# One run of 32 tiles for two attention layers with the feed-forward cut into its steps, in a gated cross-attention kernel

## What is computed

```python
x = x + tanh(g_xattn[0]) * L0_xattn(layernorm(x), ctx)        # 16 heads of 8, 77 keys, then norm, gelu FFN 512, norm
x = x + tanh(g_ffn[0])   * L0_ffn(layernorm(x))               # DEPTH = 2 local attention layers, below
x = x + tanh(g_xattn[1]) * L1_xattn(layernorm(x), ctx, trans) # 8 heads of 16, scores * trans, masked softmax
x = x + tanh(g_ffn[1])   * L1_ffn(layernorm(x))               # bf16 -> fp8 rounding, 128x128 product, bias

def _layer(x):                      # one of the two local layers, 8 heads of 64
    q, k, v = split(shift_token(x) @ wqkv)          # half of the features come from the token before
    q, k = rotary_xpos(l2norm(q) * qs, l2norm(k) * ks)
    x = x + local_attention(q, k, v) @ wo           # window of 64, looking one window back
    h = layernorm(shift_token(x)) * lg + lb
    a, g = split(h @ w1 + b1)                       # 2 * 341 hidden
    return x + (a * gelu(g)) @ w2 + b2
```

## Time and profile before

| | |
|---|---|
| median of 3 runs | 737.69 us (737.4, 740.5, 737.69) |
| the profiled execution | 737.42 us, its span 735.6 us |
| busy: PE, DVE, ACT, POOL | 584.8, 506.6, 346.6, 417.7 us |
| stage A ends, first `products` | 203.2 us |
| local layers end (last `finish`) | 591.6 us |
| second cross attention, to its last sum | 591.5 to 696.8 us |
| rounded feed-forward | 698.4 to 735.6 us |

### The profile page before, as it was taken

The page is one execution under the profiler, slowest core; times in us unless marked ns, Lnnn a source line. Parts: engine busy times, 40 slices in busy tenths (PEclk is TensorE's granted clock), DMA queues, the critical chain, the costliest instruction groups (busy, mean ns, idle before and its releaser), DMA issues. The chain is left out here.

```text
span 735.6 us, 13205 instructions
## 1 busy us (share of the span) xinstructions
PE 584.8 (79%) x4922; PEld 412.7 (56%) x4922; DVE 506.6 (69%) x1117; ACT 346.6 (47%) x603; POOL 417.7 (57%) x342
## 2 busy tenths in 40 slices
PE   4679999689289999998699899999968955768511
PEld 3337777557136777777465466777754623555400
DVE  1868888646777888875644778888655336676496
ACT  2235554363356666664534566566535323343221
POOL 5536674272289999990312999999513015555320
PEclk9559999979698999999999999999999966789955
DMA  7600000000011111110000111111100000000001
GB/s 254 182 1 1 1 1 1 1 1 1 0 43 29 31 31 31 40 29 2 1 1 14 30 47 30 32 30 32 24 1 1 1 0 0 0 1 1 1 0 57
DMA packets 16141, 18.15 MB, mean 25 GB/s; under 512 B 4261, under 2 KB 10831, under 8 KB 16079
## 3 DMA queue, kind: packets, MB, share of 16 engines
q1 hardware_dynamic: 14639, 14.70, 7.8%
q10 hardware_dynamic: 1440, 2.61, 1.1%
HBM read 8.01 MB, written 1.05 MB: 12 GB/s over the span
## 5 line engine op out<-in xcount | busy, mean ns | idle before, releaser
L222 POOL TENSOR_TENSOR rstd<-rstd,minus_half 128x4 f32<-128x4 f32 x32 | 34.1, 1065 | 162.6 <-DVE rstd L216 162.6
L1295 POOL TENSOR_TENSOR qk<-qk 128x512 f32<-128x512 f32 x64 | 80.2, 1274 | 33.8 <-DVE qk L1181 33.8
L1299 POOL TENSOR_TENSOR rn<-n,minus_half 128x16 f32<-128x16 f32 x32 | 93.8, 2931 | 2.7
L1178 DVE TENSOR_TENSOR qk<-ps,rt 128x512 f32<-128x512 f32 x64 | 44.0, 688 | 45.1 <-ACT sq L1099 31.2
L1137 ACT ACTIVATE ptb<-ps 128x512 f32<-128x512 f32 x64 | 34.8, 595 | 72.5 <-PE ps L902 72.5
L1304 POOL TENSOR_TENSOR qk<-qk,rn 128x512 f32<-128x512 f32 x64 | 65.4, 1044 | 2.5
L610 POOL TENSOR_TENSOR xy<-xy,rd 128x616 f32<-128x616 f32 x32 | 38.9, 1217 | 39.9 <-DVE rd L479 39.9
L1099 ACT ACTIVATE sq<-ps 128x512 f32<-128x512 f32 x64 | 37.7, 598 | 20.8 <-PE ps L865 7.6
L1423 POOL TENSOR_TENSOR vv<-vv,mx 128x616 f32<-128x616 f32 x16 | 19.9, 1243 | 44.5 <-DVE mx L1385 44.5
L563 PE MATMUL ps<-pt,vbd_a 128*128 128x128 f32 x320 | 39.5, 279 | 6.8 <-ACT pt L577 6.8
L872 PEld LDWEIGHTS ps<-consts,qk 128*128 128x128 f32 x256 | 29.3, 141 | 27.0 <-issue 16.1
(11 more groups left out here) (200 smaller groups left out, 1631.6 us busy)
## 6 DMA issues: line engine op xcount, KB each, us to landing
vv<-vv SPq DMA_DIRECT2D x62, 130.0 KB, 2.3
wqkv<-in_wqkv SPq DMA_DIRECT2D x1, 1536.0 KB, 16.8
x<-in_x SPq DMA_DIRECT2D x4, 256.0 KB, 8.7
out<-xy SPq DMA_DIRECT2D x4, 256.0 KB, 2.3
w_b<-in_w_b SPq DMA_DIRECT2D x1, 682.0 KB
tmat<-in_tmat SPq DMA_DIRECT2D x1, 616.0 KB, 7.7
w<-in_w ACTq DMA_DIRECT2D x1, 512.0 KB, 3.9
rot<-in_c_rot ACTq DMA_DIRECT2D x1, 512.0 KB, 8.4
```

The lines of the kernel that those rows point to most:

```text
L1178: dve.tensor_tensor(qk[:, n % 3, kind].rearrange("p (h d) -> p h d", d=DH), src.rearrange("p (h d) -> p h d", d=DH), rt[:, layer, j, i:i + ...
L1295: pool.tensor_tensor(w, w, qk2[:, kind], ALU.add).then_inc(done, 1)
L1299: pool.tensor_tensor(rn[:, k, :], n2[:, k, :], minus_half[:], ALU.pow).then_inc(rn_done, 1)
```

## The change

The two local layers become one run of steps over NT2 = 32 tiles (tile n is tile n mod 16 of layer n // 16). The feed-forward of group g (0 to 7) is cut into pieces that lie inside steps: statistics at step 9 + 4g, norm and transposition at 10 + 4g, one chunk of hidden values in each of steps 11, 12, 13 + 4g, projection and `finish` at 14 + 4g; the transposition of y for the next group (`turn`) lies in the step before its first tile. The pieces use banks 4 and 5 (and 2, 3 for one chunk), `hidt` and `gel` have one buffer (in `qt`), and a chunk waits for the one before it. The token shift is made by SP with three copies a group into `hs` (`move`) in place of matmuls; all four norms of a group are ACT's. Stage A no longer finishes groups 1 to 3: DVE, POOL and ACT do the rest of it (`add_ffn(3)`, `add_x(2)`, `add_x(3)`, `norm_y(1)` to `(3)`) at the ends of steps 0 to 2. Waits for weights (`LFFN_IN`) move ahead of step 0.

In the second cross attention DVE takes the maxima of tile n before the masking of tile n - 1, PE makes the scores of tile n + 1 first in a step, and ACT takes exp right after the copy of the transposed weights. In the rounded feed-forward `quantise` has six operations for eight, and the scaling ahead of it is ACT's, into two buffers `qs`.

```diff
-    v.do(dve.tensor_scalar(t.bitcast(U32), r.bitcast(U32), 0x7FFFFFFF, None, ALU.bitwise_and))
+    v.do(dve.tensor_scalar(t, r, OVER, None, ALU.mult))
     v.sync()
-    v.do(dve.tensor_scalar(t, t, 448.0, 448.0, ALU.max, ALU.subtract))
-    v.sync()
-    v.do(dve.tensor_scalar(t, t, 3e38, 0.0, ALU.mult, ALU.mult))
-    v.sync()
-    ins = dve.tensor_tensor(dst, r, t, ALU.add)
+    ins = dve.scalar_tensor_tensor(out=dst, in0=t, scalar=0.0, in1=r, op0=ALU.mult, op1=ALU.add)
...
-                        add_ffn(0)
-                        add_ffn(1)
-                        add_x(0)
-                        add_ffn(2)
...
+                        add_ffn(dve, 0)
+                        add_x(dve, 0)
+                        add_ffn(dve, 1)
+                        norm_y(dve, 0)
+                        add_x(dve, 1)
+                        add_ffn(dve, 2)
...
-                hidt = qk[:].rearrange("p a k d -> p (a k d)").rearrange("p (k c s) -> p k c s", k=2, c=NH)
-                gel = pb[:].rearrange("p k h q -> p (k h q)")[:, 0:2 * S].rearrange("p (k s) -> p k s", k=2)
-                for layer in range(DEPTH):
+                hidt = qt[:].rearrange("p u s -> p (u s)")[:, 0:NH * S].rearrange("p (c s) -> p c s", c=NH)
+                gel = qt[:, U - 1, :]
+                hs = wa1[:].rearrange("p (j d) -> p j d", d=D)
+                FLIP, HIDDEN, PROJECT = 10, 11, 14
...
+                    def due(n, at):
+                        g, r = divmod(n - at, TPB)
+                        return g if r == 0 and 0 <= g < U2 else None
+                    def chunk(n):
+                        g, c = divmod(n - HIDDEN, TPB)
+                        return (g, c) if c < NH and 0 <= g < U2 else None
...
+                            if chunk(n) is not None:
+                                pe.wait_ge(qt_done, min(n - LS + 1, NT2))
+                                pe.wait_ge(kt_done, min(n - LS + 1, NT2))
+                                pe.wait_ge(ont_done, min(n - LO, NT2))
...
+                                hidden(*chunk(n))
+                            if due(n, PROJECT) is not None:
+                                pe.wait_ge(qt_done, min(n - LS + 1, NT2))
+                                project(due(n, PROJECT))
+                            turned_now = n < NT2 - 1 and n % TPB == TPB - 1
+                            if turned_now:
+                                pe.wait_ge(q_prod, n + 1)
+                                turn((n + 1) // TPB, bank_q)
...
+                                if chunk(n) is not None:
+                                    pe.wait_ge(hid_done, chunks(n))
+                                if due(n, PROJECT) is not None:
+                                    pe.wait_ge(y_done, done_by(n, PROJECT))
+                                pe.matmul(bank_c, tokens(n), wqkv[:, n // NT, 2 * INNER:3 * INNER], start=True,
+                                          stop=True).then_inc(v_raw, 1)
...
+                        def move(g):
+                            t0 = TPB * (g % U)
+                            sp.wait_ge(r_done, TPB * (g + 1))
...
+                            sp.dma_start(hs[1:P, :, 64:128], y[0:P - 1, t0:t0 + TPB, 64:128]).then_inc(hs_in, 16)
+                            sp.dma_start(hs[0:1, 1:TPB, 64:128], y[P - 1:P, t0:t0 + TPB - 1, 64:128]).then_inc(hs_in, 16)
+                            sp.dma_start(hs[:, :, 0:64], y[:, t0:t0 + TPB, 0:64]).then_inc(hs_in, 16)
...
+                            if LP <= n < NT2 + LP:
+                                m = n - LP
+                                act.wait_ge(s_used, m + 1)
+                                e = pb[:, m % 2, :, :]
+                                act.activation(e, e, ACT.Exp).then_inc(exp_done, 1)
+                            if due(n, FLIP) is not None:
+                                norm(due(n, FLIP))
+                            if chunk(n) is not None:
+                                gelu(*chunk(n))
+                            if n < NT2 - 1 and n % TPB == TPB - 1:
+                                turned((n + 1) // TPB, bank_q)
...
+                            if chunk(n) is not None:
+                                hidden(*chunk(n))
...
+                            if due(n, PROJECT) is not None:
+                                finish(due(n, PROJECT))
+                            if due(n, FLIP - 1) is not None:
+                                stats(due(n, FLIP - 1))
+                            if n == 0:
+                                norm_y(dve, 1)
+                                add_ffn(dve, 3)
+                                add_x(dve, 2)
+                            if n == 1:
+                                norm_y(dve, 2)
+                                add_x(dve, 3)
+                            if n == 2:
+                                norm_y(dve, 3)
...
                         def round8(u):
-                            dve.wait_ge(xbf_dve, 2 * (u + 1))
-                            dve.wait_ge(xbf_act, 2 * (u + 1))
-                            v.do(dve.tensor_scalar(qf[0][:], xbf[:, sl(u), :].rearrange("p n d -> p (n d)"), rscale[:, 0:1], None,
-                                                   ALU.mult))
-                            v.sync()
-                            quantise(dve, v, qf, xq[:, sl(u), :].rearrange("p n d -> p (n d)"), S, xq_done)
+                            dve.wait_ge(scaled, u + 1)
+                            quantise(dve, v, (qs[u % 2], *qf), xq[:, sl(u), :].rearrange("p n d -> p (n d)"), S, xq_done)
```

More of the change, by code:

```diff
@@ L44 @@
 RING = 6
+OVER = 7.3e35
 HIDT_AT = 13472
@@ L634, in flamingo_kernel, with add_ffn, add_x, norm_y @@
                 hidt = sb("hidt", [P, 2, NC, S], scope=scope)
[L636 to L639, removed]
+                with stage("a_chain", "x_chain", "ap_chain", "var1", "rstd1", "var2", "rstd2", "var3", "rstd3", "nmr1", "nmr3", "xn_dve", "axn_act",
+                           "axnt_raw", "axnt_done", "h_raw", "h_done", "a_proj", "f_used", "a_base", "yn_dve", "yn_act") as (block, sems):
+                    (a_chain, x_chain, ap_chain, var1, rstd1, var2, rstd2, var3, rstd3, nmr1, nmr3, xn_dve, axn_act,
+                     axnt_raw, axnt_done, h_raw, h_done, a_proj, f_used, a_base, yn_dve, yn_act) = sems
+                    xv = []
+                    def add_ffn(dve, u):
+                        dve.wait_ge(a_proj, u + 1)
+                        dve.wait_ge(a_base, u + 1)
+                        ins = dve.tensor_tensor(base[:, sl(u), :], bank[6 + u % 2].rearrange("p (j d) -> p j d", d=D),
+                                                base[:, sl(u), :], ALU.add)
+                        ins.then_inc(f_used, 1)
+                        dve.wait_ge(f_used, u + 1)
+                        dve_stats(dve, xv[0], u, base, var2)
+                    def add_x(dve, u):
+                        for n in range(TPB * u, TPB * (u + 1)):
+                            xv[0].do(dve.scalar_tensor_tensor(out=base[:, n, :], in0=base[:, n, :], scalar=mv[:, n, 0:1],
+                                                          in1=gated_rows[:, 0, :], op0=ALU.subtract, op1=ALU.mult))
+                        xv[0].sync()
+                        dve.wait_ge(rstd2, u + 1)
+                        for n in range(TPB * u, TPB * (u + 1)):
+                            xv[0].do(dve.scalar_tensor_tensor(out=x[:, n, :], in0=base[:, n, :], scalar=rstd[:, n:n + 1],
+                                                          in1=x[:, n, :], op0=ALU.mult, op1=ALU.add))
+                        xv[0].sync()
+                        dve_stats(dve, xv[0], u, x, var3)
+                    def norm_y(dve, u):
+                        dve.wait_ge(rstd3, u + 1)
+                        dve_nmr(dve, u, nmr3)
+                        for n in (TPB * u, TPB * u + 1):
+                            dve_norm(dve, n, y[:, n, :], x[:, n, :]).then_inc(yn_dve, 1)
+                    def norm_y_rest(act, u):
+                        act.wait_ge(nmr3, u + 1)
+                        for n in (TPB * u + 2, TPB * u + 3):
+                            act_norm(act, n, y[:, n, :], x[:, n, :]).then_inc(yn_act, 1)
@@ L1522, in _ @@
                                                ACT.Copy).then_inc(pt_done, 1)
+                            if n < NT:
+                                act.wait_ge(sh_done, n + 1)
+                                act.activation(sh[:, n % 2, :], sh[:, n % 2, :], ACT.Exp, scale=DC ** -0.5).then_inc(exp_done, 1)
                             if n < NT and ahead(n, 2) is not None:
@@ L1532, in _ @@
                                 norm(ahead(n, 1))
-                            if n < NT:
-                                act.wait_ge(sh_done, n + 1)
-                                act.activation(sh[:, n % 2, :], sh[:, n % 2, :], ACT.Exp, scale=DC ** -0.5).then_inc(exp_done, 1)
         with region():
@@ L1628, in _ @@
                         norm(0)
+                        scale(0)
```

(3 more changed lines are left out.)

986 lines of the change are left out of this document (463 added, 523 removed).

## The result

The changed kernel takes 748.0 us (median of four runs, 744.8 to 749.9) against 737.9 before: ratio 1.0125, interval 1.0081 to 1.0170. It is slower by 10 us where 52 us less were forecast. The profiled execution took 744.81 us, its span is 743.0 us.

A forecast was written before the change was run, and what follows sets the result against it. Local layers: POOL bounds the first steps, PE every later one. Gains of 15.9 (start), 20.1 (steps and drain), 10 (second cross attention) and 5.6 us (rounding) sum to 51.6: 737.4 to 685.8 us, range 668 to 716.

The forecast's parts named there:

- The copies into `hs`: Local layers, each group: SP's three copies take 3.8 us, hidden in the steps, exposed in the drain.
- some 5 us: Full steps: DVE asks for the copies only at the step's end, some 5 us after they land.
- The rival of the copies: Three copies take 7 us; `stats`, next products and POOL wait, 8 times 2.5 us: 706 us, chance 0.08.
- Steps 0 to 10: First local steps: POOL 3.9 us late, regains 0.45 a step, 1.6 left at tile 11; 85.3 us for 83.7.
- Steps 11 to 30: Full local steps: PE bounds, loads and chunk's way covered; 42.6 us a group, 213 for five (208 to 235).
- Drain: End of local layers, once instead of twice: 47 us to the last `r_done`, then group 7; 70 (60 to 80).
- the clock: Drain, group 7 alone: 1 us for a PE clock falling in waits; at half clock up to 8 more.
- Second cross attention: Exp moved up shrinks DVE's waits; four tiles 20.4 us instead of 23.77; 10 us saved (-3 to 25).
- the shorter copy of outputs: Second cross attention, PE: scores now cover this copy instead of that of weights; a plain step 3.9 us.
- Rounding: Rounded feed-forward: DVE never idle, fewer operations save 1.4 us a group, four times, 5.6 us.
- The start: End of stage A: first product at 187.2 us, 15.9 us earlier (between 0 and 19).
- The rival in which more is gained: Second cross attention reaches DVE's floor, 15 us more, and the drain 64: 667 us, chance 0.10.

The follow-up runs named there:

- the copy mended: Changed kernel with the shifted copy of 127 partitions issued as two, of 112 and 15: 713.9 us, ratio 0.967 to the kernel before.
- the runs with tanh: Tanh in place of gelu in the local feed-forward: on the changed kernel 747.5 us (1.0107); with the copy in two pieces 716.0 us (0.9686).
- the two runs with the kernel before: Kernel before plus second cross attention's new orders: of ACT, DVE and PE, 734.2 us (0.9964); of ACT and DVE alone, 730.9 us (0.9914).
- the kernel with the work spread out: Against the kernel with the copy in two pieces and PE's old order (0.9615): stage A's moved work over steps 0 to 7; 716.6 us, 0.9715.

## Why the prediction was wrong

**The copies into** `hs` are the step that failed. It took the landing time of a copy of 128 partitions for one of 127, and held the copies for hidden behind "some 5 us". They take 9.8 us (3.8 with 112 partitions, and 4.8 as four copies of which two are of 112 and 15), and DVE stands for them eight times, 4.7 us on the mean and 7.53 us in the drain's last group. With the copy mended, the profiled local layers fall from 419.8 to 389.7 us and the time by 34. This alone turns 24 us of gain into 10 of loss. The rival of the copies had the place right (DVE in `stats`, then the products), and the forecast weighed it at 0.08 with 7 us for the three copies and 2.5 us a group. Its reason, strips of 256 bytes, is not the cause: the strips are the same in all these kernels. The 127 partitions stood in the diff, and no rival named them.

**Steps 0 to 10.** The forecast let POOL's lateness be the cost and POOL regain it. POOL was indeed late, by 4.4 us at tiles 2 to 7, but more was lost on DVE: tile 1 starts 11.6 us after tile 0 instead of 4.8 (in the kernel before 208.05 less 203.21), PE stands for it and, back at 1.2 GHz after the gap (granted clock 0.50 from 200 to 204 us), makes its next product, two records, in 2.07 us in place of 1.02:

```profile
200.06 2.07 PE L879 MATMUL ps<-wqkv,ht 128*128 128x512 f32 x2 [8.44 <-DVE qk L1198]
```

DVE's first product is 8.8 us late at tile 2, against the kernel before, 8.4 at tile 4 and 9.0 at tile 9. Nothing is regained, for from tile 4 on each of these products waits for ACT's square of what PE has just made, and POOL has no rest up to tile 7. The pace of PE, on which POOL was to catch up, had itself been set back. With the copy in two pieces 94.9 us are left of the 99.4, against 85.3 forecast. That is 11.3 us late at tile 11, of which 9.0 are there at tile 9 and 2.2 are DVE's wait for the first group's copies; of the 16.1 us by which the first product came earlier, 7 remain at tile 9 in the changed kernel.

**Steps 11 to 30.** With the copy mended a group has 44.32 us for the 42.6 forecast, and tile 31 stands 221.6 us behind tile 11 for 213. The terms that were mis-sized: PE's added work is 9.8 us (busy 42.78 in place of 32.99), not 8.9, and the value product waits 1.5 us for `finish`, not 0.6 (2.3 in the changed kernel, five times). Moving `finish` showed that this wait is real and can go. That PE bounds, that DVE and POOL keep up, and that the table loads and the way of a chunk through gelu and DVE are covered, was right; the runs with tanh show it for the loads, and the period in which PE is busy throughout, once `finish` is moved, for the rest.

**Drain.** 83.7 us for 70. From the last tile's first product to its last `r_done` it is 52.0 us in the changed kernel and 46.3 with the copy mended (47 forecast). Group 7 alone takes 31.7 and, mended, 26.8 us for the 23.1 of the sum. The mended 26.8 are 4.8 for the copies (3.8 in the sum), 5.7 to the transposition, as forecast, 2.3 from there to the first chunk (1.4), 10.4 for the three chunks (7.8, and 1 for the clock), 3.0 and 0.7 for projection and `finish`. DVE still stands 2.66 us for the copies, and after this wait PE makes the first chunk's two products at half clock (granted clock 0.50), in 2.04 and 1.91 us, in both kernels within 0.01. Drain of the changed kernel, timeline of PE:

```profile
592.85 2.04 PE L943 MATMUL ps<-xt,w_b 128*128 128x512 f32 x2 [1.18 <-ACT xt L1130]
594.69 1.91 PE L945 MATMUL ps<-xt,w_b 128*128 128x512 f32 x2
```

**Second cross attention.** 2.4 us in the profile, 2.7 alone, for 10. DVE's wait for exp went as argued. What failed is the sentence that the scores cover "the shorter copy of outputs" as well as they had covered that of the weights: it costs 3.7 us by the two runs with the kernel before. Without it 6.3 us are gained and a group of four tiles takes about 21.9, not 20.4.

**Rounding.** 27.9 us from the first statistics to the last store's operation in place of 33.7, so 5.8 for 5.6; alone 4.9, with an interval of 2.8 to 7.1. Right.

**The start** was right to 0.1 us, in part by luck: its terms as written add up to 187.0 and not 187.2, and behind the same code the first product stands anywhere between 186.2 and 190.7 us in the profiles of these experiments. Rows 2 of the kernel before are of tiles 0, 7, 11 and the last, not 6 and 10 as labelled; the 8.27 us a step and 83.7 us for eleven steps taken from them hold. The rival in which more is gained comes to 665 by its terms (685.8 less 15 and 6), not 667.

Together, against the profiled run: 51.5 us of the local layers and 7.6 of the second cross attention, less 0.2, are the 59 us between 685.8 and 744.8. Of the 51.5 the copy has 30, the first steps 10, the full steps 9 and the drain 3. The range ended at 716: the kernel with the copy mended lies in it, at 714, but near its end. Only the first steps were missed by more than their bounds: 0 to 6 us late at tile 11, and 11.3 measured. The full steps (221.6 in 208 to 235), the drain (73.1 in 60 to 80) and the second cross attention (2.4 in -3 to 25) lie within theirs, each on the slow side.

The best kernel tried, with the copy in two pieces, PE's old order in the second cross attention, `finish` ahead and the moved work in pieces, runs at 701.2 us, 4.8% (4.5 to 5.1) under before. The merged layers do gain; one copy's partition count undid it.

## What to carry to other kernels

Price a DMA by its own shape: a row of a copy with 128 partitions says nothing on one with 127, and a slow copy also holds the issues behind it on its queue. Work moved into a loop that one engine fills is free only in pieces smaller than the slack of the engine that gets it, and in these runs what the engine that bounds had lost was not regained. An order that removes one engine's wait should be tried without the reorderings on the others, as here PE's took back 3.7 of the 6.3 us that ACT's and DVE's gave.

## What the runs showed of the hardware

A copy of 127 partitions holds the next issue on the same queue for 6.45 us, even one of 0.8 KB, and it and the two copies behind it have landed 9.8 us after its issue, at a busy share of 0.08 of the 16 DMA engines; with 112 partitions the next issue takes 0.73 us, the three copies 3.8 us, and the share is 0.56.

DVE and POOL seem to stretch each other. Steps 0 and 1 of the changed kernel on DVE, then step 0 on POOL:

```profile
194.70 2.58 DVE L659 SCALAR_TENSOR_TENSOR x<-base,rstd,x 128x128 f32<-128x128 f32 x4
...
204.20 1.14 DVE L659 SCALAR_TENSOR_TENSOR x<-base,rstd,x 128x128 f32<-128x128 f32 x4
```

```profile
194.39 2.23 POOL L1340 TENSOR_TENSOR qk<-qk,rn 128x512 f32<-128x512 f32 x2
```

Four operations of the same form, of two groups, take 2.58 us beside POOL's products and 1.14 beside its power of 128x16. Two of the first four take 1.01 and 1.13 us, the other two 0.33 and 0.34. In step 2 of the kernel with the work spread out the 3.50 us of line 654 stand beside POOL's sums. In the second cross attention the new order lets DVE's masking and POOL's subtraction fall together, and they grow by 181 and 438 ns each. The Trainium skill says so much ("GPSIMD Engine Reference", section "Specifications"): the interfaces to SBUF are shared, and operations of VectorE with two SBUF inputs contend. These operations have two such inputs, so the trace agrees; that the overlap is the cause was read from the trace and not tested by a run.

Of 38 table loads of 1283 ns 37 were taken away without a change in the time (748.0 and 747.5 us; 713.9 and 716.0 with the copy mended). Behind a load between exp and gelu in the changed kernel the next operation starts 0.01 or 0.02 us after its end, or where it had to wait for PE, 0.20 to 0.36 us.
